# Deformable convolution on one core: the ninth tap of an eighth chunk computed by TensorE, with a second copy of the transposed table, one record buffer, and the projection ahead of the first turn

## The reference, cut to what matters

```python
x = x + L0(gn(x))     # 1x1 to 128 channels; 3x3 depthwise with kernels made from the pooled image;
                      # y * tanh(softplus(y)); 1x1 back to 64 channels
x = x + L1(gn(x))     # deformable 3x3, below
offset = conv2d(x, w_off, b_off)                       # 18 numbers a pixel: where each of 9 taps looks
mask = sigmoid(conv2d(x, w_mask, b_mask))              # 9 a pixel
val = gather(iy0, ix0) * (wy0 * wx0)[:, None] + gather(iy0, ix0 + 1) * (wy0 * wx1)[:, None] \
    + gather(iy0 + 1, ix0) * (wy1 * wx0)[:, None] + gather(iy0 + 1, ix0 + 1) * (wy1 * wx1)[:, None]
val = val * mask[:, None]
xd = jnp.einsum('bikhw,oik->bohw', val, w_def)
z = einsum(concat([xd, offset, mask]), w_1x1) + b_1x1  # then batch norm and silu
```

## Time and profile before

| | |
|---|---|
| median of 3 runs | 5559.13 us (5555.79 to 5571.62) |
| profiled execution, its own time | 5569.03 us |
| span of that execution | 5567.2 us |
| PE (TensorE matmul) busy | 4232.8 us, 76% |
| DVE (VectorE) busy | 4433.4 us, 80% |
| ACT (ScalarE) busy | 2478.1 us, 45% |
| POOL (GpSimd) busy | 4109.3 us, 74% |
| mean granted TensorE clock | 0.779 of full speed |

### The profile page before, as it was taken

How to read it: one execution, slowest core, us unless ns; L and a number is a source line. 1 busy time by engine, 2 the same in 40 slices (tenths; PEclk the granted TensorE clock), 3 DMA queues, 4 the chain that set the end, 5 groups by cost and what they waited for, 6 DMA issues and landing times.

```text
span 5567.2 us, 43350 instructions
## 1 busy us (share of the span) xinstructions
PE 4232.8 (76%) x13878; PEld 1852.8 (33%) x13878; DVE 4433.4 (80%) x5166; ACT 2478.1 (45%) x3420; POOL 4109.3 (74%) x4307
## 2 busy tenths in 40 slices
PE   8586777777777787777877778787787777778682
PEld 3233333333333333333333333333333333333231
DVE  5887869779697887978879797786978878788664
ACT  3354445445444444445544454454444444445221
POOL 1777777777777777777777777777777777777776
PEclk8686868879687786878868688696877868778685
DMA  4334344443534435344343443435344353433433
GB/s 106 103 118 135 106 132 122 126 130 112 143 106 133 122 111 140 107 132 123 120 135 106 132 123 123 132 107 148 107 130 123 111 144 107 132 115 119 122 108 100
DMA packets 284052, 675.58 MB, mean 121 GB/s; under 512 B 77215, under 2 KB 119082, under 8 KB 281578
## 3 DMA queue, kind: packets, MB, share of 16 engines
q0 software_dynamic: 206400, 563.88, 33.9%
q1 hardware_dynamic: 77424, 108.93, 7.7%
HBM read 618.39 MB, written 54.12 MB: 121 GB/s over the span
## 4 chain that ended last, share of the span: by engine, by line
DVE 29%; POOL 28%; PE 26%; issue 13%; DMA 3%; ACT 1%; DVEq 0%; POOLq 0%; ACTq 0%; SPq 0%
POOL gat L505 28%; PE yo_ps L771 14%; DVE conv_ps L1237 7%; DVE gat L1367 5%; DVE pairs L1346 5%; DVE hat_s L1394 3%; DMA gat<-patch_table,ixu 3%; PE z_ps L696 3%; PE tap_ps L690 2%; DVE hat_wy L1401 1%; DVE xb L1258 1%; PE conv_ps L569 1%; DVE stat L1260 1%; PE xh_ps L754 1%; DVE conv_ps L1234 1%
## 5 line engine op out<-in xcount | busy, mean ns | idle before, releaser
L505 POOL DMA_INDIRECT gat<-patch_table,ixu x4300 | 4101.3, 954 | 1445.6 <-issue 1292.9
L771 PE MATMUL yo_ps<-hat_s,hat_image 128*128 128x512 f32 x3080 | 1660.9, 694 | 472.4 <-DVE hat_wy L1401 453.4
L1367 DVE TENSOR_TENSOR gat<-gat,wgt_ps 128x1024 f32<-128x1024 f32 x1075 | 1303.2, 1215 | 635.3 <-DMA gat<-patch_table,ixu 629.0
L1346 DVE TENSOR_REDUCE pairs<-gat 128x256 f32<-128x1024 f32 x1024 | 1239.7, 1211 | 0.0
L771 PEld LDWEIGHTS yo_ps<-hat_s,hat_image 128*128 128x128 f32 x3080 | 659.4, 223 | 1372.8 <-issue 871.5
L1035 ACT ACTIVATE val<-tap_ps 128x512 f32<-128x512 f32 x512 | 303.5, 593 | 1100.1 <-PE tap_ps L690 1099.7
L690 PE MATMUL tap_ps<-ident,pairs 128*128 128x128 f32 x2048 | 395.6, 325 | 470.4 <-DVE pairs L1346 470.3
L1237 DVE SCALAR_TENSOR_TENSOR conv_ps<-xh,kb,conv_ps 128x1024 f32<-128x1024 f32 x480 | 617.6, 1287 | 12.7
L690 PEld LDWEIGHTS tap_ps<-ident,pairs 128*128 128x128 f32 x2048 | 266.9, 163 | 759.5 <-DVE pairs L1346 618.3
L696 PE MATMUL z_ps<-val,w_pair 128*64 128x256 f32 x2048 | 425.2, 502 | 10.2 <-ACT val L1035 2.1
L645 PE MATMUL conv_ps<-np,w_om 128*41 128x512 f32 x1440 | 394.3, 706 | 39.4 <-ACT cat L994 39.4
(11 more groups left out here) (235 smaller groups left out, 4452.5 us busy)
## 6 DMA issues: line engine op xcount, KB each, us to landing
gat<-patch_table,ixu POOLq DMA_INDIRECT x4300
xb<-in_x SPq DMA_DIRECT2D x31, 1024.0 KB, 9.8
patch_table<-rec SPq DMA_DIRECT2D x120, 256.0 KB, 2.4
hat_image<-patch_table SPq DMA_DIRECT2D x144, 128.0 KB
out<-n_z SPq DMA_DIRECT2D x128, 128.0 KB
patch_table<-np SPq DMA_DIRECT2D x2, 1072.5 KB
patch_table<-gat SPq DMA_DIRECT2D x8, 256.0 KB, 2.2
patch_table<-rec SPq DMA_DIRECT2D x16, 97.0 KB
```

The lines of the kernel that those rows point to most:

```text
L505: pool.indirect_dma_start(gat[:, k, t * 2 * REC:(t + 1) * 2 * REC], None, table_rows, bass.IndirectOffsetOnAxis(ixu[:, i, k, t:t + 1], 0)) ...
L771: m = pe.matmul(hat_sum[:, :], hat_image[:, i, t, :], hat_s[:, i, :], start=(i == 0), stop=(i == HI - 1))
L1346: dve.tensor_reduce(total, gat[:, k, :].rearrange("p (t x c h) -> p t c x h", t=TILES, x=2, h=2), mybir.AxisListType.XY, ALU.add).then_inc ...
L1367: dve.tensor_tensor(patch, patch, wk.rearrange("p (n h) -> p n h", h=2).unsqueeze(2).to_broadcast([128, TILES * 2, C, 2]), ALU.mult).then_ ...
```

## The change

It does five things.

1. Tap 8 is computed in chunk 7 as well: of image 0 the chunks are now 3, 4, 7, of the others 0 to 4 and 7, 93 chunks in place of 77.
2. `hat_image` has two copies, by the image's parity, so the ten loads no longer wait for the last turn of the image before.
3. `rec` is one buffer in place of two. ScalarE waits before each of its copies until the one before has been stored.
4. In `plan_of` the chunk's own plan comes first among equal units, then the turns, then what prepares the next computed tap.
5. The scratch space in SBUF for the descriptors of GpSimd's DMAs is set to 8192 bytes a partition.

```diff
-HATS0 = (3, 4)
-HATS = (0, 1, 2, 3, 4)
+HATS0 = (3, 4, 7)
+HATS = (0, 1, 2, 3, 4, 7)
...
-    return by_unit(PLAN_NEXT_HAT[0:1] if has_hat(q + 1) else (), PLAN_HAT[0:2] if has_hat(q) else (), plan,
-                   PLAN_HAT[2:] if has_hat(q) else (), PLAN_NEXT_HAT[1:] if has_hat(q + 1) else ())
+    return by_unit(plan, PLAN_HAT if has_hat(q) else (), PLAN_NEXT_HAT if has_hat(q + 1) else ())
...
-        hat_image = sb("hat_image", [128, HI, HT, REC])
+        hat_image = sb("hat_image", [128, 2, HI, HT, REC])
...
-        rec = sb("rec", [128, 2, TILES, REC])
-        rec_l = rec[0:LAST, 1, 0:2, :].rearrange("p t d -> p (t d)")
+        rec = sb("rec", [128, TILES, REC])
+        rec_l = rec[0:LAST, 0:2, :].rearrange("p t d -> p (t d)")
...
-                if hats_before(n * NCH):
-                    sp.wait_ge(hat_mm, HT * hats_before(n * NCH))
+                if n > 1:
+                    sp.wait_ge(hat_mm, HT * hats_before((n - 1) * NCH))
...
-                    m = pe.matmul(hat_sum[:, :], hat_image[:, i, t, :], hat_s[:, i, :], start=(i == 0), stop=(i == HI - 1))
+                    m = pe.matmul(hat_sum[:, :], hat_image[:, q // NCH % 2, i, t, :], hat_s[:, i, :], start=(i == 0), stop=(i == HI - 1))
...
                 act.wait_ge(tr_mm, n * NCH + (c + 3))
-                act.wait_ge(rec_out[c % 2], (n * (NCH // 2) + c // 2) * 16 + 16)
-                if c == 1:
+                if c == 0:
                     act.wait_ge(last_out, n * 16 + 32)
+                else:
+                    act.wait_ge(rec_out[(c - 1) % 2], (n * (NCH // 2) + (c - 1) // 2) * 16 + 32)
...
-    nc = bacc.Bacc("TRN2", target_bir_lowering=False, num_devices=1)
+    nc = bacc.Bacc("TRN2", target_bir_lowering=False, num_devices=1, dynamic_dma_scratch_size=8192)
```

More of the change, by code:

```diff
@@ L393, in store_chunk @@
                 dst = table_rows[bass.ds((n % 2) * (TR * PW) + c * CH, CH), :].rearrange("(p t) d -> p (t d)", t=TILES)
-                sp.dma_start(dst, rec[:, c % 2, :, :].rearrange("p t d -> p (t d)")).then_inc(rec_out[c % 2], 16)
+                sp.dma_start(dst, rec[:, :, :].rearrange("p t d -> p (t d)")).then_inc(rec_out[c % 2], 16)
             def first_chunk(c):
@@ L416, in load_hat_image @@
                     src = table[row:row + 2 * t - 1:2, 1:1 + W, :].rearrange("t x d -> x t d")
-                    sp.dma_start(hat_image[C * upper:C * upper + C, i, 0:t, :], src).then_inc(hat_in, 16)
+                    sp.dma_start(hat_image[C * upper:C * upper + C, n % 2, i, 0:t, :], src).then_inc(hat_in, 16)
             def store_out(b, g):
@@ L488, in _ @@
             pool.wait_ge(cleared, 2)
-            pool.memset(hat_image[C:, HI - 1, 1:, :], 0.0).then_inc(cleared, 1)
+            pool.memset(hat_image[C:, :, HI - 1, 1:, :].rearrange("p s t d -> p s (t d)"), 0.0).then_inc(cleared, 1)
             pool.wait_ge(border_out, 32)
@@ L966, in to_table @@
                 act.wait_ge(tr_mm, n * NCH + (c + 3))
-                act.wait_ge(rec_out[c % 2], (n * (NCH // 2) + c // 2) * 16 + 16)
-                if c == 1:
+                if c == 0:
                     act.wait_ge(last_out, n * 16 + 32)
-                act.activation(rec[:, c % 2, :, :].rearrange("p t (c h) -> p t h c", h=2),
+                else:
+                    act.wait_ge(rec_out[(c - 1) % 2], (n * (NCH // 2) + (c - 1) // 2) * 16 + 32)
+                act.activation(rec[:, :, :].rearrange("p t (c h) -> p t h c", h=2),
                                tr_ps[:, :].rearrange("p (t h c) -> p t h c", t=TILES, h=2), ACT.Copy).then_inc(rec_done, 1)
```

## The result

The changed kernel takes 5626.36 us (median of 4 runs, 5612.0 to 5632.1), the kernel before, beside it on the same chip, 5565.38 us (4 runs, 5555.79 to 5583.91). The ratio is 1.010, with a 95% interval of 1.0079 to 1.0121. It is slower, on the side that was forecast and inside the range, by some 2.5 times what was forecast (61 us for 24). The profiled execution took 5624.92 us, with a span of 5623.1 us against 5567.2 us: 55.9 us more.

The account below looks back on a forecast made before the run. GpSimd's issue of gathers bounds it, at the limit where chunks 7 to 3 take 226.1 us. +5.3 - 2.6 - 0.6 = +2.1 us over fourteen images, less 5 for the first, is +24: 5583 us on the 5559.1 median, range 5575 to 5650.

Parts of the forecast that it names:

- The limit on S: While chunks 7, 0, 1, 2, 3 take up to 226.1 us, GpSimd sets the time; above it each us costs one.
- S: Summed time of chunks 7, 0, 1, 2, 3 in an image: 226.1 us before, forecast to change by +2.1 us.
- Chunk 7: With four turns added, the chunk grows from 50.2 to 55.5 us, +5.3; its steps sum to 56.6.
- Turn 0: First turn of chunk 7, behind x_mean on TensorE: takes 7.3 us and ends at t = 9.5.
- The root: In chunk 7's x_var, ScalarE's root follows the hat_y copy: ready at about 13.7, 2.1 us later than VectorE asks.
- `hat_post` 0: VectorE's step in chunk 7 that comes with hat_part: moves from t = 14.6 to 16.7.
- taken at full clock: TensorE's queue in chunk 7 after turn 1 ends at 24.7: hardly a pause, full clock, 31.9 us to the next first multiply.
- two lower cases: Chunk 7 at 54.4 us if only the root is on time, or 51.7 if turns 0 and 1 both run at full clock.
- Chunk 0: VectorE's waits of 0.95 and 1.68 us there go: -2.6 us, the chunk at 40 to 42.
- The projection ahead of the turn: VectorE's waits for the projection, 17.4 us in all or 1.2 an image, go; taken as -0.6 us an image.
- The rival by which a smaller scratch stops GpSimd: Half the descriptor space lets only one gather be under way: pace from 1.25 to about 2 us, kernel over 8000; chance 0.02.
- The rival that TensorE warms up: Turns bring full clock in chunk 7: it takes 51.7 us, the kernel 5499; decides under about 53 us; chance 0.27.

Follow-up runs that it names:

- thin: The change with two of five matmuls in each of chunk 7's four turns: 5550.74 us against 5568.83 for the kernel before, 0.9964.

## Why the prediction was right, and where its sum was off

**The limit on S: right on the side that was reached.** It was read from two images of the kernel before, as 226.1 us with an image of 268 gathers x 1.2545 = 336.2 us, so that the rest of an image is 110.1. The runs have 111 there, from S = 225.8 to 233.0. To images 1 to 14 the gathers saved in chunk 7 were worth nothing, as forecast: how far VectorE's first multiply is behind the fourth gather of its chunk rose at chunk 0 from 9.9 to 21.3 us (means), and from chunk 2 on it stands at 26 to 27 us, where the ring of places is full and GpSimd stops. In before it comes to 25.3, in chunk 4. The waits were to go "from 42 to some 130 us" and went to 218, since S rose by more.

**Chunk 7: right in its steps, short in the sum.** TensorE's timeline in chunk 7 of the changed kernel, from 1127.47 (t = 0):

```profile
1129.66 7.24 PE L770 MATMUL yo_ps<-hat_s,hat_image 128*128 128x512 f32 x10
...
1144.69 6.56 PE L770 MATMUL yo_ps<-hat_s,hat_image 128*128 128x512 f32 x10 [2.87 <-DVE hat_wy L1401]
...
1154.10 2.68 PE L547 MATMUL conv_ps<-hcx,kg_w 128*128 128x1 f32 x18
1156.71 1.12 PE L695 MATMUL z_ps<-hat_wy,w_hat 128*64 128x256 f32 x4
1157.76 6.85 PE L770 MATMUL yo_ps<-hat_s,hat_image 128*128 128x512 f32 x10
...
1172.17 6.25 PE L770 MATMUL yo_ps<-hat_s,hat_image 128*128 128x512 f32 x10
```

and VectorE's in the same stretch, the waits of which the prediction spoke:

```profile
1141.04 0.16 DVE L1184 RECIPROCAL mr<-std 64x1 f32<-64x1 f32 x1 [1.11 <-ACT std L876]
1143.95 0.69 DVE L1401 TENSOR_TENSOR hat_wy<-yo_ps,hat_wy 128x512 f32<-128x512 f32 x1
...
1156.81 0.17 DVE L1193 TENSOR_TENSOR kb<-conv_ps,kg_b 128x9 f32<-128x9 f32 x1 [2.58 <-PE conv_ps L547]
1164.65 0.69 DVE L1401 TENSOR_TENSOR hat_wy<-yo_ps,hat_wy 128x512 f32<-128x512 f32 x1 [5.28 <-PE yo_ps L770]
1178.47 0.69 DVE L1401 TENSOR_TENSOR hat_wy<-yo_ps,hat_wy 128x512 f32<-128x512 f32 x1 [8.39 <-PE yo_ps L770]
...
1184.63 0.69 DVE L1408 TENSOR_TENSOR n_z<-n_z,xb 64x512 f32<-64x512 f32 x1 [2.18 <-ACT n_z L1045]
```

- Turn 0 was to end at t = 9.5 and ends at 9.4, in 7.24 us for 7.3.
- The root was to be ready at 13.7, 2.1 us late; VectorE takes it at 13.6, after 1.11 us.
- `hat_post` 0 comes at t = 16.5 for 16.7, and turn 1 begins at 17.2 for 17.4, after a pause of 2.87 us for 3. It ends at 23.8 for 24.7, in 6.56 us for 7.3.
- From there on the queue was "taken at full clock", and this is **the term that was mis-sized**: turns 2 and 3, put at 4.5 each, ran 6.85 and 6.25, together 4.1 us more. The kernel's matmuls took 2.68 for 3.6. VectorE's wait before the last `hat_post` was to be "5 us or more" and is 8.39.
- The end came at t = 58.1, for 56.6 by the sum and 55.5 as I took it between two cases. Of the two lower cases neither came: the root was late, and turn 1 ran slow. The queue behind turn 1 took 34.3 us for 31.9: the two turns 4.1 more, the kernel's matmuls 0.9 less, the other steps together 0.8 less; and turn 1 had ended 0.9 early. That the sum missed by 1.5 and not by 4 is so in part luck. Over the images chunk 7 has 57.3 us in the mean.

**Chunk 0: right, but its base was one image.** The forecast of 40 to 42 us holds (40.4). The gain is 1.4 us in the mean and not 2.6, because the image I read took 43.4 us there where before's mean is 41.8.

**The projection ahead of the turn: zero, not -0.6.** VectorE's waits for it went from 17.4 us in 13 to 5.0 in 2, but chunks 1 to 3 take 134.3 us for 134.5, and the run with the old order shows no gain of the new one. Where chunk 7 is left as it was, the rest of the change costs 0.21%. Since the scratch alone costs nothing and a second record buffer brings nothing, that leaves the order or the second copy of the image. The chunk means do not show where it lies (chunks 4 and 5 are shifted against each other, 30.2 and 33.7 us for 31.6 and 32.2), and neither was tried alone, so this 0.2% has no cause here.

So S rose by 6.2 - 1.4 - 0.2 = +4.6 us for a forecast +2.1, of which 0.9 is chunk 7, 1.2 chunk 0 and 0.4 chunks 1 to 3. 14 x 4.6 = +64, measured +66.7; the first image gave 7.7 for 5, and the last 3.1 for nothing.

**What was put at nothing** was nothing: the record buffer (two of them: the same time), the scratch (1.0002), chunk 6 (47.0 us for 47.5 in the means), the pace of the gathers. The rival by which a smaller scratch stops GpSimd fell by a run of its own. That the scratch holds 512 descriptors, an estimate from the Trainium skill ("DMA: Bandwidth & Descriptors", Terms and SWDGE), no run here shows; that 8192 bytes of it cost nothing, the pace of 1.250 us does.

**The rival that TensorE warms up** was half right: the clock of chunk 7 rose from 0.50 to 0.79, but the turns that buy it cost more than it brings. That "the default state is throttled, and activity releases the throttle" (the Trainium skill, "TensorE: Matmul & The Clock Gate", Part 1) agrees with the chunk's clock under no, thin and full turns: 0.50, 0.63, 0.79 (means over images 2 to 13: 0.51, 0.67, 0.80); the last section has a stretch where the clock fell all the same. It did not make the change faster. The point from which the rival decides, given as "chunk 7 stays under about 53 us", held: with the root first and the kernel's matmuls early it takes 52.0, and that kernel is faster than before.

## What to carry to other kernels

Where a producer runs ahead of its consumers through a ring of places, cut the period at the consumer and find the stretch in which it falls behind. Once that stretch is over the limit, less work for the producer is worth nothing, and the stretch's length counts one for one. New work on an engine with much idle time is priced by its place in that engine's queue, by what stands behind it and who waits there: one entry of the order moved by one place was worth as much here as the whole change cost. And take the base of each term from the mean over the periods, not from the one that was looked at.
